# The context loop's matmul operands at eight different offsets within 512 bytes, instead of all at the same one

## The reference

```python
# cross attention, x normalised by a layer norm; ctx is [25088, 512]
scores = (Q(x) @ K(ctx).T) * scale            # 256 x 25088
char2sub = softmax(scores) @ V(ctx)           # 256 x 512
sub2char = interpolate(softmax(Q(ctx) @ K(x).T * scale) @ V(x), 256)
gate = sigmoid(concat(char2sub, sub2char) @ Wg.T + bg)
x = x + gate * char2sub + (1 - gate) * sub2char
x = x + self_attention(layernorm(x))          # 16 heads, half-causal mask
x = x + experts(layernorm(x))                 # a shared expert and 32 routed ones, top 1
```

## Time and profile before

| what | value |
|---|---|
| median of 3 runs | 1169.48 us (1167.11 to 1169.86) |
| the profiled execution | 1165.06 us, its span 1163.3 us |
| TensorE busy in the span | 1038.4 us, 89% |
| VectorE busy | 618.1 us, 53% |
| ScalarE busy | 372.8 us, 32% |
| mean granted TensorE clock | 0.971 |

### The profile page before, as it was taken

One profiled execution on the slowest core, in us unless ns is written; L12 is line 12 of the kernel. 1 busy time (PEld: TensorE's weight loads), 2 busy tenths in 40 slices (PEclk: granted clock), 3 DMA queues, 4 the chain that ended last, 5 costly groups with the idle time before them and its releaser, 6 DMA issues.

```text
span 1163.3 us, 16777 instructions
## 1 busy us (share of the span) xinstructions
PE 1038.4 (89%) x6736; PEld 714.6 (61%) x6736; DVE 618.1 (53%) x977; ACT 372.8 (32%) x546; POOL 3.5 (0%) x20
## 2 busy tenths in 40 slices
PE   9999999999999999999999999999887666667666
PEld 8867878878888888888866756454432222222223
DVE  4457878878878878878854365222121111111112
ACT  2444456546546556546433252000000000000000
POOL 1000000000000000000000000000000000000000
PEclk9999999999999999999999999999997898997989
DMA  9548799887888887888859435999999999999997
GB/s 347 188 145 301 284 350 349 305 297 282 286 296 284 285 303 278 286 298 282 287 193 384 145 145 230 428 425 425 426 426 426 428 428 428 428 428 429 426 429 308
DMA packets 91122, 381.48 MB, mean 328 GB/s; under 512 B 5584, under 2 KB 6224, under 8 KB 74064
## 3 DMA queue, kind: packets, MB, share of 16 engines
q1 hardware_dynamic: 91088, 381.00, 84.1%
HBM read 355.29 MB, written 25.69 MB: 327 GB/s over the span
## 4 chain that ended last, share of the span: by engine, by line
DMA 47%; PE 27%; DVE 17%; SPq 4%; ACT 2%; issue 2%; DVEq 0%; ACTq 0%
DMA deep<-in_r_down 23%; DMA strips<-turned 11%; DMA pt<-strips 9%; DVE nat_lo L1261 4%; DVE turned L1288 4%; PE ps L984 4%; DVE pt_lo L1266 4%; SPq L351 3%; DMA wide<-in_r_up 3%; DVE st L1273 2%; ACT pt_hi L1052 2%; PE ps L544 2%; PE ps L970 2%; PE ps L964 1%; DMA nat<-in_ctx_rows 1%
## 5 line engine op out<-in xcount | busy, mean ns | idle before, releaser
L558 PE MATMUL ps<-ctt_hi,q_hi 128*128 128x512 f32 x392 | 153.7, 392 | 0.0
L560 PE MATMUL ps<-ctt_hi,q_lo 128*128 128x512 f32 x392 | 152.6, 389 | 0.0
L559 PE MATMUL ps<-ctt_lo,q_hi 128*128 128x512 f32 x392 | 152.5, 389 | 0.0
L571 PE MATMUL ps<-nat_hi,pt_hi 128*128 128x512 f32 x368 | 143.8, 391 | 3.9 <-DVE pt_lo L1266 3.9
L573 PE MATMUL ps<-nat_hi,pt_lo 128*128 128x512 f32 x368 | 143.3, 389 | 0.0
L572 PE MATMUL ps<-nat_lo,pt_hi 128*128 128x512 f32 x368 | 143.3, 389 | 0.0
L1205 ACT ACTIVATE sg<-ps 128x256 f32<-128x256 f32 x32 | 12.3, 384 | 388.0 <-PE ps L964 388.0
L1602 DVE TENSOR_TENSOR hh<-sg,ps 128x256 f32<-128x256 f32 x32 | 13.5, 421 | 227.7 <-PE ps L970 227.7
L984 PE MATMUL ps<-deep,hh_t 128*32 128x512 f32 x496 | 77.9, 756 | 54.9 <-DMA deep<-in_r_down 53.6
L1256 DVE TENSOR_TENSOR ctt_lo<-ctt,ctt_hi 128x2048 fp32r<-128x2048 f32 x49 | 111.0, 2289 | 18.6 <-ACT ctt_hi L1044 18.2
L1048 ACT ACTIVATE nat_hi<-nat 128x2048 fp32r<-128x2048 f32 x48 | 92.1, 1918 | 79.4 <-DMA nat<-in_ctx_rows 79.4
(11 more groups left out here) (281 smaller groups left out, 1257.4 us busy)
## 6 DMA issues: line engine op xcount, KB each, us to landing
wide<-in_r_gate SPq DMA_DIRECT2D x32, 2048.0 KB, 26.0
wide<-in_r_up SPq DMA_DIRECT2D x32, 2048.0 KB, 27.4
deep<-in_r_down SPq DMA_DIRECT2D x31, 2048.0 KB, 25.8
ctt<-in_ctx_t SPq DMA_DIRECT2D x49, 1024.0 KB, 7.9
nat<-in_ctx_rows SPq DMA_DIRECT2D x48, 1024.0 KB, 7.4
strips<-turned SPq DMA_DIRECT2D x96, 256.0 KB, 5.1
pt<-strips SPq DMA_DIRECT2D x24, 1024.0 KB, 4.8
w_gate<-in_w_g_t SPq DMA_DIRECT2D x2, 1024.0 KB, 13.6
```

The costliest lines, as they stand in the source:

```text
L558: mm(o, qh, ctt_hi[par][:, c, :], start=(c == 0), stop=False)
L559: mm(o, qh, ctt_lo[par][:, c, :], start=False, stop=False)
L560: last = mm(o, ql, ctt_hi[par][:, c, :], start=False, stop=(c == HC - 1))
L571: mm(o, p_hi[:, w, :], n_hi[:, t, :], start=(first and t == 0), stop=False)
```

## The change

Only addresses change. The tiles of the loop are moved by a few hundred bytes, so that a stationary tile and the stream that it meets no longer start at the same offset within 512 bytes. Space that was free takes up the shifts; `s2c` and the tiles behind it move up by 1,536 bytes, and `pexp`, `turned` and `pt` by 2,048.

```diff
-        cursor[0] = lined = (cursor[0] + 4095) // 4096 * 4096
+        lined = (cursor[0] + 4095) // 4096 * 4096
+        cursor[0] = lined + 256
         pt_hi = place("pt_hi", [P, 2, QT * KT, P], F32R)
+        cursor[0] = lined + 8704 + 64
         q_hi = place("q_hi", [P, HC, NQ], F32R)
+        cursor[0] = lined + 13312 + 128
         q_lo = place("q_lo", [P, HC, NQ], F32R)
+        cursor[0] = lined + 17920
         s2c = place("s2c", [P, QT, D])
...
-        ctt = [at(f"ctt{k}", [P, HC, BLK], F32, LOOPB + k * kb) for k in range(2)]
-        ctt_hi = [at(f"ctt_hi{k}", [P, HC, BLK], F32R, LOOPB + (2 + k) * kb) for k in range(2)]
-        nat = [at(f"nat{k}", [P, KT, D], F32, LOOPB + (4 + k) * kb) for k in range(2)]
-        nat_hi = [at(f"nat_hi{k}", [P, KT, D], F32R, LOOPB + (6 + k) * kb) for k in range(2)]
+        col_at = [LOOPB, LOOPB + kb + 192]
+        col_hi_at = [LOOPB + 2 * kb + 512, LOOPB + 3 * kb + 704]
+        row_at = [LOOPB + 4 * kb + 1024, LOOPB + 5 * kb + 1312]
+        row_hi_at = [LOOPB + 6 * kb + 1536, LOOPB + 7 * kb + 1600]
+        prob_at = LOOPB + 8 * kb + 2048
+        ctt = [at(f"ctt{k}", [P, HC, BLK], F32, col_at[k]) for k in range(2)]
+        ctt_hi = [at(f"ctt_hi{k}", [P, HC, BLK], F32R, col_hi_at[k]) for k in range(2)]
+        nat = [at(f"nat{k}", [P, KT, D], F32, row_at[k]) for k in range(2)]
+        nat_hi = [at(f"nat_hi{k}", [P, KT, D], F32R, row_hi_at[k]) for k in range(2)]
...
-        pt_lo = at("pt_lo", [P, 2, QT * KT, P], F32R, LOOPB + 11 * kb)
+        pt_lo = at("pt_lo", [P, 2, QT * KT, P], F32R, prob_at + 3 * kb + 320)
```

More of the change, by code:

```diff
@@ L120, in perceiver_layer @@
         c2s = at("c2s", [P, QT, D], F32, small + 16384)
-        c2s_t = at("c2s_t", [P, HC, NQ], F32, lined + 32768)
+        c2s_t = at("c2s_t", [P, HC, NQ], F32, lined + 34304)
         gate = at("gate", [P, QT, D], F32, small)
@@ L171, in perceiver_layer @@
         kb = HC * BLK * 4
-        ctt = [at(f"ctt{k}", [P, HC, BLK], F32, LOOPB + k * kb) for k in range(2)]
-        ctt_lo = [at(f"ctt_lo{k}", [P, HC, BLK], F32R, LOOPB + k * kb) for k in range(2)]
-        ctt_hi = [at(f"ctt_hi{k}", [P, HC, BLK], F32R, LOOPB + (2 + k) * kb) for k in range(2)]
-        nat = [at(f"nat{k}", [P, KT, D], F32, LOOPB + (4 + k) * kb) for k in range(2)]
-        nat_lo = [at(f"nat_lo{k}", [P, KT, D], F32R, LOOPB + (4 + k) * kb) for k in range(2)]
-        nat_hi = [at(f"nat_hi{k}", [P, KT, D], F32R, LOOPB + (6 + k) * kb) for k in range(2)]
@@ L178, in perceiver_layer @@
[L178 to L185, removed]
@@ L186, in perceiver_layer @@
-        pt = at("pt", [P, G, 2, QT * KT, Q], F32, LOOPB + 10 * kb)
-        pt_lo = at("pt_lo", [P, 2, QT * KT, P], F32R, LOOPB + 11 * kb)
+        col_at = [LOOPB, LOOPB + kb + 192]
[4 more added lines that the diff above has]
+        ctt = [at(f"ctt{k}", [P, HC, BLK], F32, col_at[k]) for k in range(2)]
@@ new lines, in perceiver_layer @@
+        ctt_lo = [at(f"ctt_lo{k}", [P, HC, BLK], F32R, col_at[k]) for k in range(2)]
+        ctt_hi = [at(f"ctt_hi{k}", [P, HC, BLK], F32R, col_hi_at[k]) for k in range(2)]
+        nat = [at(f"nat{k}", [P, KT, D], F32, row_at[k]) for k in range(2)]
+        nat_lo = [at(f"nat_lo{k}", [P, KT, D], F32R, row_at[k]) for k in range(2)]
+        nat_hi = [at(f"nat_hi{k}", [P, KT, D], F32R, row_hi_at[k]) for k in range(2)]
+        end_nat = at("end_nat", [P, KT, D], F32, col_at[1])
+        end_nat_lo = at("end_nat_lo", [P, KT, D], F32R, col_at[1])
@@ new lines, in perceiver_layer @@
+        end_nat_hi = at("end_nat_hi", [P, KT, D], F32R, col_hi_at[1])
+        pexp = at("pexp", [P, 2, QT * KT, P], F32, prob_at)
+        turned = at("turned", [P, G, 2, QT * KT, Q], F32, prob_at + kb)
+        end_pt_hi = at("end_pt_hi", [P, QT * KT, P], F32R, prob_at + kb)
+        end_pt_lo = at("end_pt_lo", [P, QT * KT, P], F32R, prob_at + kb + 4096)
+        pt = at("pt", [P, G, 2, QT * KT, Q], F32, prob_at + 2 * kb)
+        pt_lo = at("pt_lo", [P, 2, QT * KT, P], F32R, prob_at + 3 * kb + 320)
@@ L189, in perceiver_layer @@
+        assert prob_at + 4 * kb + 320 <= RINGB + 6 * WB
         xn = at("xn", [P, QT, D], F32, RINGB + 10 * kb)
-        c_t = at("c_t", [P, HC, NQ], F32, lined + 16384)
-        bias2 = at("bias2", [P, NQ], F32, lined + 20480)
-        bqs_rep = at("bqs_rep", [P, HC, P], F32, lined + 21504)
+        c_t = at("c_t", [P, HC, NQ], F32, lined + 17920)
+        bias2 = at("bias2", [P, NQ], F32, lined + 22016)
+        bqs_rep = at("bqs_rep", [P, HC, P], F32, lined + 23040)
         o = RINGB + 11 * kb
@@ L205, in perceiver_layer @@
                                               enumerate(("w_qc", "w_ks", "w_kc", "w_qs", "w_vc", "sel_t")))
-        w_vs = at("w_vs", [P, HC, D], F32, LOOPB + 2 * kb)
+        w_vs = at("w_vs", [P, HC, D], F32, col_hi_at[0])
         w_gate1 = at("w_gate1", [P, HC, D], F32, LOOPB)
```

## The result

Over six runs the changed kernel took 1174.47 us in the median (1173.35 to 1176.62), the kernel before 1168.06 (1163.46 to 1169.86). The ratio is 1.0066, with a 95% interval of 1.0045 to 1.0086. The loss is real and small. The profiled execution took 1173.91 us. The ratios in this document leave out executions in the chip's slow state; there was one, 1514.75 us at a mean granted clock of 0.649, among the ten of the first experiment.

A forecast was written before the change was run, and what follows sets the result against it. TensorE was taken to bound the loop's later pairs, with the chain of other work nearly equal. 2,352 matmuls x 0 ns left the median at 1169 us (own range 1166 to 1172, outer range 1162 to 1189), chance 0.50.

The forecast's parts named there:

- What bounds the loop, and where a longer matmul would show: Context loop: TensorE is the bound in the 14 later pairs; the 7 early pairs can absorb 4.6 us in waits.
- The prediction's own formula: Cost of slower loop matmuls: 2,352 times the added ns each, less 4.6 us absorbed by the early 7 pairs.
- I take 0, because the nearest rows on offsets (float32, equal against unequal) show none: Loop's fp32r matmuls: unequal offsets priced at 0 ns, carried over from plain float32 matmuls outside the loop.
- The term that was put at 0: Weight load against stream in 2,352 fp32r matmuls: 0 ns each, bounds -10.9 and +10.9 ns.
- The doubled reading pace: Fp32r matmuls read their stream twice as fast as float32, so might be sensitive to offsets that float32 ignores.
- The second reason for 0: Loop matmuls keep 226.7 ns while DMA traffic goes from 322 to 289 GB/s and ScalarE and VectorE read the same memory.
- For most of every stream TensorE also reads a stationary tile: Loop matmuls: the next tile's load, 188 ns in the mean, runs beside each stream; matmuls start 226.7 ns apart.
- Coarse differences do nothing: Loop: stationary tiles 0, 512, 1,024 and 1,536 bytes past a multiple of 2,048 all keep 226.7 ns per matmul.
- The slower rival: Loop matmuls: with unequal offsets weight reading holds up the stream; at +10.9 ns 21 us more, 1190 us; chance 0.28.
- The faster rival: Loop matmuls: equal offsets are the collision, unequal ones save up to 10.9 ns each; 1162 to 1163 us; chance 0.16.
- The ring's rival: Loop's chain without matmuls (stores, read-back, splits, transposes): a split or load slowed by its new address, 1179 us; chance 0.06.
- What would show it: Trace of the loop: unequal matmul distances within one pair mean a rule on offsets; 226.7 ns everywhere means none.

The follow-up runs named there:

- the first experiment: All of the loop's stationary tiles and streams set 64 bytes past a multiple of 512, against the kernel before: 1166.18 against 1167.60 us, ratio 0.9987.

## Why the prediction was wrong

- **What bounds the loop, and where a longer matmul would show: right.** The early 7 pairs absorbed it by waits, the later 14 paid it in full: 1,344 matmuls x 4.7 ns = 6.3 us, measured 6.2. The prediction's own formula, 2,352 x 4.7 = 11.1 us less the 4.6 us of waits in the early pairs, gives 6.5, beside 6.4 by which the median moved, but that closeness is partly luck. At 4.7 ns the early pairs' 672 matmuls grow by only 3.2 us in all, and no more than that can be absorbed there; so the formula should give 7.9, which lies inside the interval of the ratio (5.3 to 10.0 us).
- **"I take 0, because the nearest rows on offsets (float32, equal against unequal) show none": this step failed.** Plain float32 matmuls ignore the difference, fp32r ones do not, and the prediction had called carrying over its weakest step. The term that was put at 0 measured +4.7 ns for the mix of eight differences, inside the bounds of -10.9 and +10.9 ns. The time, 1174.47 us, lies inside the outer range of 1162 to 1189, but that range had been held open for the rivals; the forecast's own 1166 to 1172 missed. The doubled reading pace, named there as the one reason for doubt, pointed the right way; that the pace is the reason is not shown, as float32 and fp32r differ in more than that.
- **The second reason for 0 was also weak.** That 226.7 ns does not move with DMA traffic or with ScalarE's and VectorE's reads is true of the kernel before. It only says that these do not disturb TensorE. It says nothing on TensorE's two own reads.
- **"For most of every stream TensorE also reads a stationary tile": not shown.** The prediction took the load's record of 188 ns for its reading time. The loads 112 ns apart beside 128-column streams leave at most that for one load, about half of a distance of 226.7 ns.
- **"Coarse differences do nothing": right, and it pointed to the rule.** 0, 512, 1,024 and 1,536 were known to be equal; the runs add 256 to that list.
- **The slower rival, "the weight load gets in the stream's way": right in sign and place, its size too large.** It was priced at +10.9 ns and 1190 us, the kernel took 4.7 ns and 1174.47 us. The worst single difference measured, 96, costs 7.5 ns.
- **The faster rival** fell: no difference tried is quicker than 0. (Its sum took 16 later pairs, where the earlier trace rows have 14; 14 give 4.8 us in place of 5.4.) **The ring's rival** fell too: the means of L1266 and L1271 (before: L1256 and L1261) stayed at 2290 and 2289 ns, ScalarE's at 1921 and 1918. Only the stores of `strips` landed later, in 5.6 us at the median in place of 5.1, but TensorE was busy for all of the later pairs' 310.99 us and waited for nothing.
- **What would show it: right.** Unequal distances within one pair were the sign named for a rule on offsets, and they are there.

By the Trainium skill (SBUF — State Buffer, Who interferes with whom) TensorE's port for the stream and its port for the weight load are independent. Taken to mean that no placing of the two operands costs time, which is how the prediction used it, the runs disagree as far as fp32r goes: the relative start of the two operands alone moves the distance from 226.7 to 234.2 ns. That the two reads collide in the memory is my reading of it, argued from the dependence on the difference, from the repeat at 256 bytes and from the settling after a disturbance; no run took a load away to show it directly, and which load meets which stream stays open.

## What to carry to other kernels

In loops of fp32r matmuls that load a new stationary tile beside each stream, put stationary tiles and streams at starts that differ by a multiple of 256 bytes (measured with 128x128 tiles and 512 columns). Neither has to be aligned to anything coarser for its own sake. The gain is up to 7.5 ns of about 234 per 512-column matmul, and it only counts where TensorE is the bound. Spreading addresses "to avoid conflicts" did the opposite here. And when a price is carried over from a neighbouring instruction form, ask first whether that form loads the suspected resource as hard: the float32 rows read their stream at half the pace, and their equality said nothing on fp32r.

## What the hardware showed that I had not expected

- The pace of fp32r matmuls depends on the difference of operand starts modulo 256 bytes: 226.7 ns at 0, 233 to 234 ns at 32 to 96 and at 160, 232 at 128, 229.6 at 192, and 232.5 to 233 at 480, the one value tried for 224.
- The dependence has no mirror symmetry (64: 233.4, 192: 229.6), and mixed offsets don't cost the mean of their parts.
- At difference 0 there remain about 11 ns per matmul, over the pace of the float32 rows, that do not shrink with the stream (174.0 ns at 384 columns).
- After a change from 128-column to 512-column streams, matmuls at difference 0 run slower (230.0 ns) for six places before they settle at 226.7.
- Weight loads follow each other at 112 ns, though their records are 190 ns long.
